# Two PSUM banks per ScalarE copy in the merges of a four-layer graph network

## The reference

```python
# layer 0 (attention), 1 (edge weights), 2 (attention by source), 3 (four heads of 64)
agg = segment_sum(h_src * attn_weights[:, None], tgt, num_segments=N)
agg = segment_sum(adj_vals[:, None] * h[edge_src], edge_dst, num_segments=N)
agg = segment_sum(feature[src] * alpha[:, None], dst, num_segments=n)
outs = [segment_sum(messages * norm[:, hd:hd + 1], dst, N) for hd in range(4)]
```

## Time and profile before

| | |
|---|---|
| runs of the kernel (us) | 8005.48, 8016.32, 8031.96 |
| median | 8016.32 |
| span of the profiled execution | 8012.0, first to last instruction |
| PE, DVE, ACT, POOL busy in it | 5871.2, 5323.9, 3367.9, 4776.0 us |
| ACT emptying copies (L1414) | 1568, 577.4 us busy, 1092.4 idle ahead of them |
| ACT seeding copies (L1401) | 1568, 587.9 us busy, 258.7 idle ahead of them |
| PE step products (L1350) | 6264 records, 1613.5 us busy, 657.7 idle ahead of them |

### The profile page before, as it was taken

How to read it: one execution, slowest core, us unless ns; L and a number is a source line. 1 busy time by engine, 2 the same in 40 slices (tenths; PEclk the granted TensorE clock), 3 DMA queues, 4 the chain that set the end, 5 groups by cost and what they waited for, 6 DMA issues and landing times. The chain is left out here.

```text
span 8012.0 us, 151569 instructions
## 1 busy us (share of the span) xinstructions
PE 5871.2 (73%) x22090; PEld 3583.1 (45%) x22091; DVE 5323.9 (66%) x17689; ACT 3367.9 (42%) x10659; POOL 4776.0 (60%) x6058
## 2 busy tenths in 40 slices
PE   4997899747779997777999877777656779500477
PEld 3773244335544443555444344444225558400365
DVE  5999888645579995455666566666864569633755
ACT  1992255314555553355444333333113567400166
POOL 1556777757632223766777677777567653577443
PEclk7996699878999999899999988898888999755799
DMA  2662000048867776787899866666016878522177
GB/s 65 211 210 60 1 1 1 1 128 274 304 216 246 249 249 211 234 292 261 317 315 313 284 198 204 203 207 191 7 61 213 286 262 229 146 55 55 55 226 237
DMA packets 801351, 1457.62 MB, mean 182 GB/s; under 512 B 134969, under 2 KB 541742, under 8 KB 801175
## 3 DMA queue, kind: packets, MB, share of 16 engines
q1 hardware_dynamic: 462518, 753.28, 28.5%
q10 hardware_dynamic: 188000, 410.91, 14.9%
q0 software_dynamic: 150656, 291.76, 12.9%
HBM read 809.86 MB, written 645.70 MB: 182 GB/s over the span
## 5 line engine op out<-in xcount | busy, mean ns | idle before, releaser
L1350 PE MATMUL merge_banks<-merge_rows,merge_mask 128*128 x6264 | 1613.5, 414 | 657.7 <-SPq L1319 448.5
L1350 PEld LDWEIGHTS merge_banks<-merge_rows,merge_mask 128*128 128x128 f32 x6264 | 1250.7, 206 | 1020.5 <-issue 839.7
L1332 DVE TENSOR_SCALAR merge_mask<-ramp,dst_at,soft_at_step 128x128 f32<-128x128 f32 x2349 | 849.6, 368 | 932.3 <-PE merge_banks L1350 808.2
L1491 POOL DMA_INDIRECT merge_rows<-h,merge_take_i x1224 | 1173.4, 959 | 491.0 <-issue 314.9
L2047 PE MATMUL node_p_out<-w,node_h_t 128*128 128x259 f32 (+2 forms) x4704 | 1434.4, 428 | 11.1 <-ACT node_h_t L2086 10.3
L1414 ACT COPY merge_total<-merge_banks 128x256 f32<-128x256 f32 x1568 | 577.4, 369 | 1092.4 <-PE merge_banks L1350 937.7
L1960 POOL TENSOR_TENSOR node_inv_std<-node_var,node_minus_half 128x4 f32<-128x4 f32 x392 | 448.0, 1143 | 885.4 <-DVE node_var L1897 570.6
L2047 PEld LDWEIGHTS node_p_out<-w,node_h_t 128*128 128x128 f32 x4704 | 744.7, 191 | 263.4 <-issue 210.0
L2025 PE MATMUL node_p_turn<-ident,node_xn 128*128 128x128 f32 x3136 | 620.0, 280 | 191.6 <-DVE node_xn L1854 92.8
L2047 PE MATMUL node_p_out<-w,node_kept_t 128*128 128x512 f32 x1568 | 741.1, 595 | 0.0
L2025 PEld LDWEIGHTS node_p_turn<-ident,node_xn 128*128 128x128 f32 x3136 | 403.6, 141 | 741.5 <-issue 455.1
(11 more groups left out here) (555 smaller groups left out, 10748.7 us busy)
## 6 DMA issues: line engine op xcount, KB each, us to landing
merge_held<-own ACTq DMA_DIRECT2D x196, 512.0 KB, 6.2
x<-merge_total ACTq DMA_DIRECT2D x196, 512.0 KB, 4.3
node_x<-x SPq DMA_DIRECT2D x196, 512.0 KB, 6.1
node_x<-in_x SPq DMA_DIRECT2D x194, 512.0 KB
h<-node_rows_h SPq DMA_DIRECT2D x98, 512.0 KB
merge_held<-h ACTq DMA_DIRECT2D x98, 512.0 KB, 6.4
mix<-merge_total ACTq DMA_DIRECT2D x98, 512.0 KB, 4.3
node_mixed<-mix SPq DMA_DIRECT2D x98, 512.0 KB, 3.8
```

The lines of the kernel that those rows point to most:

```text
L1332: ins = nc.vector.tensor_scalar(mask[j][:], k.ramp[:, 0:P], columns(k.dst_at, s), columns(weight, s), ALU.is_equal, ALU.mult)
L1350: nc.tensor.matmul(banks[:, bass.ds(nc.s_assert_within(at[2 * j + 1], 0, (BANKS - 1) * 512, skip_runtime_bounds_check_because=small), D)], ...
L1491: nc.gpsimd.indirect_dma_start(rows[:, (j + n) * D:(j + n + 1) * D], None, table, bass.IndirectOffsetOnAxis(take_i[:, j + n:j + n + 1], 0) ...
```

## The change

In the merges `bank` becomes `two_banks`: one ACT instruction reads or writes 256 columns in each of two neighbouring banks. `flush` and `seed` go over pairs of tiles, count their semaphores (`kept`, `seeded`) by two, and wait for the steps of the second tile of a pair. `flush_at` keeps only the numbers of the odd tiles, so it is half as long, in the plan, in DRAM and in each merge, and one load of counts brings half as many. PE, DVE, POOL and SP keep their instructions in the merges.

```diff
@@ plan
-    flush_at = ph.sb("flush_at", [1, NT], I32)
+    flush_at = ph.sb("flush_at", [1, NT // 2], I32)
...
-                ins = nc.vector.tensor_scalar(flush_at[:, CT * q:CT * (q + 1)], left[0:1, at:at + CT], moved[0:1, 0, q:q + 1], None,
-                                              ALU.subtract)
+                pairs = CT // 2
+                ins = nc.vector.tensor_scalar(flush_at[:, pairs * q:pairs * (q + 1)], left[0:1, at + 1:at + CT:2],
+                                              moved[0:1, 0, q:q + 1], None, ALU.subtract)
@@ merge
-            def bank(q, g):
+            def two_banks(q, g):
                 first = q.side * G + g
-                return banks[:, first * 512:first * 512 + D]
+                return banks[:, first * 512:(first + 2) * 512].rearrange("p (n f) -> p n f", n=2)[:, :, 0:D]
 
             def seed(q, g):
                 if g == 0:
                     act.wait_ge(held_got[q.held], 16 * (q.held_uses + 1))
-                nc.scalar.copy(bank(q, g), held[q.held][:, g, :]).then_inc(seeded, 1)
+                nc.scalar.copy(two_banks(q, g), held[q.held][:, g:g + 2, :]).then_inc(seeded, 2)
...
                 if q.w % 4 == 0:
-                    at[:] = counts(act, flush_at, H * G, min(4, TURN - q.w) * G)
+                    at[:] = counts(act, flush_at, H * (G // 2), min(4, TURN - q.w) * (G // 2))
                 ahead = q.later(2)
-                for g in range(G):
-                    act.wait_ge(steps, at[q.w % 4 * G + g])
+                for g in range(0, G, 2):
+                    act.wait_ge(steps, at[(q.w % 4 * G + g) // 2])
                     if g == 0 and not (q.fixed and q.total_uses == 0):
                         act.wait_ge(put[q.total], q.stored(q.total_uses))
-                    nc.scalar.copy(total[q.total][:, g, :], bank(q, g)).then_inc(kept, 1)
+                    nc.scalar.copy(total[q.total][:, g:g + 2, :], two_banks(q, g)).then_inc(kept, 2)
                     if not ahead.end:
-                        act.wait_ge(kept, H * G + g + 1)
+                        act.wait_ge(kept, H * G + g + 2)
                         seed(ahead, g)
```

More of the change, by code:

```diff
@@ L1033, in plan @@
     needs = ph.sb("needs", [1, HALF // 2, 2], I32)
-    flush_at, free_at, edge_at = ph.sb("flush_at", [1, NT], I32), ph.sb("free_at", [1, V], I32), ph.sb("edge_at", [1, V], I32)
+    flush_at, free_at, edge_at = ph.sb("flush_at", [1, NT // 2], I32), ph.sb("free_at", [1, V], I32), ph.sb("edge_at", [1, V], I32)
     p_row, p_col, p_edge, p_free = (ph.ps(n, [P, 512]) for n in ("p_row", "p_col", "p_edge", "p_free"))
@@ L1268, in merge @@
     places, needs = ph.sb("places", [1, 2 * (K + 1)], I32), ph.sb("needs", [1, (K + 1) // 2], I32)
-    flush_at, free_at = ph.sb("flush_at", [1, NT], I32), ph.sb("free_at", [1, V], I32)
+    flush_at, free_at = ph.sb("flush_at", [1, NT // 2], I32), ph.sb("free_at", [1, V], I32)
     edge_at = ph.sb("edge_at", [1, V], I32)
@@ L2735, in gnn_kernel @@
         k.plan = [nc.dram_tensor(n, (1, w), I32).ap() for n, w in
-                  (("places", 2 * k.K + 2), ("needs", (k.K + 1) // 2), ("flush_at", k.NT), ("free_at", k.V), ("edge_at", k.V))]
+                  (("places", 2 * k.K + 2), ("needs", (k.K + 1) // 2), ("flush_at", k.NT // 2), ("free_at", k.V), ("edge_at", k.V))]
         h0, ends0 = dram("h0", (k.NP, D)), dram("ends0", (k.NP, 2))
```

## The result

The changed kernel took 7985.3 us in the median, the kernel before 8017.5: ratio 0.9952, 95% interval 0.9936 to 0.9969. A second set of runs, taken with the experiments, gave 7967.2 against 8010.9, ratio 0.9945 (0.9932 to 0.9959). So the gain is 38 to 44 us, where 99 were forecast.

What follows compares the result with a forecast made beforehand. Late merge turns were taken as bound by ACT's sequence, early ones by gathers; 36 us from the last merge plus 63 from the other three, 99 in all, gave 8016.3 - 99 = 7917 us, range 7890 to 7950 (0.50).

Steps and rivals of the forecast that it cites:

- What ACT is spared: ACT's merge copies and loads of counts: 0.77 us a group, 10.8 a turn, plus 2 a turn for counts; 12.8 less.
- PE's floor: PE in the merges: 4.39 us per eight steps, so 57.1 us for a turn of 104 steps, 52.7 for 96.
- The last merge, 36 us: Last merge, PE next bound: turns 4 to 6 gain 5, 8, 6; 2 and 3 5 and 5.5; first 3, last 3.5.
- The other three, 63 us: First three merges, DMA engines next bound: 21 us gained a merge, mostly turns 3 to 5; turn 6 gains 0.5.
- The DMA share: First three merges' late turns: full share taken as 0.96; turns 3 to 6 then need 68, 65, 63 and 60.7 us.
- The jump's wait: Rival: nine ACT loop-jump waits of 5 us vanish, 15 to 25 reach the end, about 7897; 0.17, shared with DMA limiting less.
- DMA takes it back: Rival: packets slow when ACT issues closer; three merges gain 5 us each, the last 25: 7976; chance 0.19.
- No gain from the copies: Rival: a two-bank ACT copy takes 0.73 us, so only counts gain, 2 us a turn: 7998; chance 0.08.
- PE starves for banks: Rival: pairs return later, costing PE up to 0.9 us a group; at half the groups 8093; chance 0.06.
- SyncE's wait for seeds: Sign: in turn 5 SyncE's wait for ACT's seeding copies falls from 53 us to under 30.
- The merges' sum does not fall to about 2120: Sign of being wrong: the four merges' total does not fall from 2218 us to about 2120.
- Anything outside them moves by over 10 us: Sign of being wrong: any part of the program outside the four merges moves by over 10 us.

Runs made afterwards that it cites:

- the edit on PE: Changed kernel with PE waiting for `clear` only at every fourth step: 7907.6 us, 0.9859; the same edit in the kernel before: 7980.5 us, 0.9953.
- with four banks: Changed kernel with PE's fewer waits, one copy for all four banks of a group and added increments keeping ACT's loops in reach: 7923.1 us, 0.9889.

## Why the prediction was wrong

The direction was right and the size was not: 99 us forecast, 38 to 44 measured. The terms in their order:

- **What ACT is spared.** The copies were right (0.585 and 0.59). But a group in the first merge's turn 5 takes 2125.20 - 2121.85 = 3.35 us in the rows below, not 3.09: from the first emptying to the second 1.19 (1.145 forecast), from there to the next group's 2.16, so that the longer second seed does not lie wholly beside the issues. That is some 3.5 us a turn less than forecast, if the other groups are like this one. The counts gave 2.1 to 2.5 us a turn for 2 (54 to 37 us in the first merge).

```profile
2121.85 0.59 ACT L1415 COPY merge_total<-merge_banks 128x512 f32<-128x512 f32 x1 [2.92 <-issue]
...
2123.04 0.58 ACT L1415 COPY merge_total<-merge_banks 128x512 f32<-128x512 f32 x1
...
2125.20 0.59 ACT L1415 COPY merge_total<-merge_banks 128x512 f32<-128x512 f32 x1 [0.91 <-PE merge_banks L1351]
```

- **PE's floor: the step that failed.** "Eight steps take 3.72 us and 0.67 for the next addresses, 4.39": the row was right, but I took the one row for every period and added 1 to 2 us a turn. In turns 4 to 7 of the last merge the mean period is 4.8 us, in turn 4 it is 5.1, with 10 of its 13 periods at 5.2 to 5.5. Nor were the 0.67 us the price of the addresses alone: with three of four waits out of PE's queue the same loads leave no pause (the 32 steps in one piece above). The trace of before held the warning: in the same turns 14 of 47 of PE's loads took over 1.5 us, and two rows of PE in its turn 4 read

```profile
7776.18 3.72 PE L1350 MATMUL merge_banks<-merge_rows,merge_mask 128*128 x16 [1.53 <-SPq L1319]
...
7784.98 3.72 PE L1350 MATMUL merge_banks<-merge_rows,merge_mask 128*128 x16 [0.65 <-DVE merge_mask L1330]
```

I had quoted one pause and did not ask for the spread of all.

- **The last merge, 36 us: 16 to 19 measured.** Turn 4 gained nothing where 5 were forecast, turn 2 gained 0 to 2 for 5, turn 7 lost 0 to 2 for a gain of 3.5; turn 6 gained 3 for 6, turn 5 gained 6.5 for 8. It is PE's queue: with its spare waits out the same change gains 48 us in this merge, and without the store's stretch of the loads turns 2 to 5 took 229 us for my 234.
- **The other three, 63 us: 28 and 34 measured**, with six jump waits gone that the forecast did not count. The turns that fell short are 2, 3, 4 and 7. With PE's waits taken out, 7 falls to 48 to 52 us, and the three gain 64 us against before. That is what was forecast, but by luck: half of it comes from an edit that the forecast did not have. Turns 3 to 6 were put at 826 - 50 = 776 us and stop at 781 to 795 whatever was relieved.
- **The DMA share.** I took 0.96 as full. Turns 5 and 6 of the first merge show 1.00 at 340 and 350 GB/s. The 358 GB/s of the Trainium skill (DMA: Bandwidth & Descriptors, Specifications) were nearer than my row, but it did not matter for the sum: turn 5 went to 57.7 for the 63 forecast, the shares in turns 5 and 6 of the next two merges are 0.89 to 0.97, and PE's relief does not shorten turns 4 to 6 of the first merge (182.6 us changed, 188.9 with the edit on PE). That the DMA engines hold these turns, as forecast, fits the shares, but no run tests it.
- **The rivals.** The jump's wait did go, in two merges of three. Its price of 15 to 25 us for nine was right in the kernel before (20), but in the changed kernel the waits make no difference that can be measured. DMA takes it back: no for its reason, since the first merge's turn 5 moved 340 GB/s where it had moved 295 and fell by 11 us; its 7976 comes nearest to the result by luck. No gain from the copies: nearly true in the result, for another reason, since their price was right and the next bound was nearer. PE starves for banks: no, 0.9998; with four banks it does.
- **What would show it.** SyncE's wait for seeds fell from 53.1 to 23.9 us in turn 5 of the first merge, as said, but in the last merge it stayed at 42.6. "The merges' sum does not fall to about 2120" came true: it was 2176 and 2167. "Anything outside them moves by over 10 us" came true as well, by 21 us in one execution and 6 in the other, but equal code outside the merges moves by up to 23 between executions, so this sign could tell nothing.

The rows of turn 5, waits of SyncE's queue in the first and the last merge:

```profile
SPq L1320 <- ACT merge_banks L1402: 23.9, 13, 4.0
...
SPq L1320 <- ACT merge_banks L1402: 42.6, 19, 5.0
```

## What to carry to other kernels

Before a faster engine is priced, cost the next bound's queue, not its array: count the instructions between two matmuls, and take the median and the maximum of every register load in it, over all turns. A wait that can never hold (here three of four waits on a count that rises by four) is not free on an engine whose queue is the bound: taking three of four out gave the changed kernel more than the change had. And an edit that only changes the number of instructions can remove or create waits at a loop's jump elsewhere, so look at those before crediting the edit.

## What the hardware did that was not expected

- PE's load of 16 addresses into registers takes 1.11 us, and mostly 1.9 to 2.2 when it begins 0.4 to 1.3 us behind ACT's issue of a 512 KB store; from 2.4 us on it takes 1.11 again. The store's bytes do it, not its issue, nor the number of its rows (512 or 128).
- ACT's own load of 8 counts, right behind its store, takes 1.5 us in the last merge, 0.73 where the stores are cut to one row, 0.55 where both transfers are gone.
- Through that, PE and ACT can lock into step: PE releases ACT, ACT's store meets PE's next load, and every period is 5.3 us for 4.39, with no engine and no DMA queue full (PE busy 46 of 63 us, DMA share 0.71).
- A jump back on ACT waits 3.9 to 6.6 us or 0.2, by where the loop lies in ACT's code: 12 added instructions took three waits of 5 us away.
- A copy over four banks of 256 columns each takes 1.01 us, over two 0.585, over one 0.367.
